# Causal scores as one full float32 product per chunk, instead of three passes over split operands

## The reference

```python
q = rope(x @ Wq.T); k = rope(x @ Wk.T); v = x @ Wv.T
scores = einsum('bhnid,bhnjd->bhnij', qc, kc)        # i, j within a chunk
decay = where(i >= j, exp(G[i] - G[j]), 0)
y_intra = (scores * decay) @ (v * dt)
y_inter = (qc * exp(G)) @ state                       # state from the chunks before
y = rmsnorm(y_intra + y_inter) * gnorm_w * silu(x @ Wg.T)
out = y @ Wo.T
```

## Time and profile before

| what | value |
|---|---|
| median of three runs | 1941.15 us (1938.84 to 1943.4) |
| profiled execution, its own time | 1941.0 us |
| its span, first to last instruction | 1939.2 us |
| TensorE busy | 1832.8 us |
| VectorE busy | 1270.4 us |
| ScalarE busy | 693.4 us |
| GpSimd busy | 643.0 us |

### The profile page before, as it was taken

The page is one execution under the profiler, slowest core; times in us unless marked ns, Lnnn a source line. Parts: engine busy times, 40 slices in busy tenths (PEclk is TensorE's granted clock), DMA queues, the critical chain, the costliest instruction groups (busy, mean ns, idle before and its releaser), DMA issues. The chain is left out here.

```text
span 1939.2 us, 27787 instructions
## 1 busy us (share of the span) xinstructions
PE 1832.8 (95%) x8856; PEld 1482.9 (76%) x8856; DVE 1270.4 (66%) x2340; ACT 693.4 (36%) x2186; POOL 643.0 (33%) x741
## 2 busy tenths in 40 slices
PE   6799999999999999999999999999887999999997
PEld 5588777777777777777777778777766888888885
DVE  7777777787777777777777777777764333333332
ACT  4533443343344434334444434343443112112111
POOL 3444444444444444443444444344400010110100
PEclk9899999999999999999999999999988999999998
DMA  4132332223232223323322232322454322323321
GB/s 153 50 99 83 91 93 70 67 98 92 82 90 94 71 66 93 95 83 91 93 63 70 87 104 77 94 64 63 135 174 155 99 83 81 98 81 92 98 76 33
DMA packets 111073, 173.54 MB, mean 89 GB/s; under 512 B 8016, under 2 KB 45904, under 8 KB 110928
## 3 DMA queue, kind: packets, MB, share of 16 engines
q1 hardware_dynamic: 110928, 171.80, 29.6%
HBM read 133.50 MB, written 38.27 MB: 89 GB/s over the span
## 5 line engine op out<-in xcount | busy, mean ns | idle before, releaser
L84 PE MATMUL p_proj<-wg_hi,shared 128*128 128x512 f32 x1024 | 362.8, 435 | 0.0
L84 PE MATMUL p_proj<-shared,wq_hi 128*128 128x512 f32 x992 | 340.5, 405 | 20.3 <-DVE rope_b L105 20.3
L113 POOL TENSOR_TENSOR q<-rope_a,rope_b 128x512 f32<-128x512 f32 x128 | 165.8, 1295 | 348.8 <-DVE rope_b L105 248.8
L84 PEld LDWEIGHTS p_proj<-wg_hi,shared 128*128 128x128 f32 x1024 | 194.2, 190 | 85.5 <-issue 46.5
L911 ACT ACTIVATE tanh<-p_proj 128x512 f32<-128x512 f32 x128 | 76.6, 599 | 488.5 <-PE p_proj L84 488.5
L84 PEld LDWEIGHTS p_proj<-shared,wq_hi 128*128 128x128 f32 x992 | 189.5, 191 | 69.4 <-DVE rope_b L105 25.5
L84 PE MATMUL p_proj<-wg_lo,shared 128*128 128x512 f32 x512 | 203.3, 397 | 0.0
L84 PE MATMUL p_proj<-shared,wq_lo 128*128 128x512 f32 x496 | 198.6, 400 | 0.0
L84 PE MATMUL p_proj<-shared,wkv_hi 128*128 128x512 f32 x496 | 169.4, 402 | 18.3 <-DVE rope_b L105 18.3
L687 PE MATMUL p_y<-v_tok,probs 128*128 128x128 f32 x1024 | 182.1, 275 | 0.0
L904 ACT ACTIVATE probs<-g_row,stab 128x128 f32<-128x128 f32 x512 | 164.6, 406 | 33.2 <-POOL g_row L1018 33.2
(11 more groups left out here) (181 smaller groups left out, 3711.3 us busy)
## 6 DMA issues: line engine op xcount, KB each, us to landing
g_row<-g_scratch SPq DMA_DIRECT2D x128, 256.0 KB, 6.0
z_scratch<-z_st SPq DMA_DIRECT2D x256, 128.0 KB
w_raw<-z_scratch SPq DMA_DIRECT2D x63, 512.0 KB, 5.9
e_row<-e_scratch SPq DMA_DIRECT2D x96, 256.0 KB, 3.9
w_raw<-in_wq_t SPq DMA_DIRECT2D x16, 512.0 KB, 8.2
w_raw<-in_wg_t SPq DMA_DIRECT2D x16, 512.0 KB, 5.6
w_raw<-in_wo_t SPq DMA_DIRECT2D x11, 512.0 KB, 5.8
w_raw<-in_wkv_t SPq DMA_DIRECT2D x8, 512.0 KB, 5.0
```

The source lines that it names most:

```text
L84: mm = pe.matmul(out, lhs[a], rhs[e], start=(i == 0 and j == 0), stop=(i == len(pairs) - 1 and j == 2))
L113: pool.tensor_tensor(out, keep["rope_a"][:, s, :], keep["rope_b"][:, s, :], ALU.add).then_inc(keep["roped"], 1)
```

## The change

The three products of `scores` become one product of float32 operands, read from `k` and `q` where GpSimd wrote them. The copies and subtractions that split q and k (`q_high`, `k_high`, `q_low`, `k_low`), their buffers and their four semaphores go. `scores` waits for `roped` itself, at chunk 0 of a step, for all five tiles. All else stays in its order.

```diff
-        q_part = [sb(f"q_{e}", [P, HG, C], F32R) for e in ("hi", "lo")]
-        k_part = [sb(f"k_{e}", [P, L], F32R) for e in ("hi", "lo")]
...
-            def scores(n, c):
+            def scores(n, b, c):
                 m = NC * n + c
                 if c == 0:
-                    pe.wait_ge(k_lo_set, n + 1)
+                    pe.wait_ge(roped, ROPED * (n + 1))
                 wait_ge(pe, probs_set, m)
-                pe.wait_ge(q_lo_set, m + 1)
                 at = slice(c * C, (c + 1) * C)
-                wide(pe, p_score[:, :, :], [([w[:, at] for w in k_part], [w[:, :, :] for w in q_part])]).then_inc(score_done, 1)
+                pe.matmul(p_score[:, :, :], k[:, b % 2, at], q[b % 2][:, :, at], start=True, stop=True).then_inc(score_done, 1)
...
-            def k_low(n, b):
-
-                dve.wait_ge(k_hi_set, n + 1)
-                dve.tensor_tensor(k_part[1][:, :], k[:, b % 2, :], k_part[0][:, :].bitcast(F32), ALU.subtract).then_inc(k_lo_set, 1)
-
-            def q_low(n, b, c):
-
-                dve.wait_ge(q_hi_set, NC * n + c + 1)
-                dve.tensor_tensor(q_part[1][:, :, :], q[b % 2][:, :, c * C:(c + 1) * C], q_part[0][:, :, :].bitcast(F32),
-                                  ALU.subtract).then_inc(q_lo_set, 1)
...
-            def q_high(n, b, c):
-                if c == 0:
-                    act.wait_ge(roped, ROPED * (n + 1))
-                wait_ge(act, score_done, NC * n + c)
-                act.activation(q_part[0][:, :, :], q[b % 2][:, :, c * C:(c + 1) * C], ACT.Copy).then_inc(q_hi_set, 1)
-
-            def k_high(n, b):
-                act.wait_ge(roped, ROPED * n + 1)
-                wait_ge(act, score_done, NC * n)
-                act.activation(k_part[0][:, :], k[:, b % 2, :], ACT.Copy).then_inc(k_hi_set, 1)
```

More of the change, by code:

```diff
@@ L478, in attention_stage @@
         masked_set, xw_set = sem("masked_set"), sem("xw_set")
-        q_hi_set, q_lo_set, k_hi_set, k_lo_set = sem("q_hi_set"), sem("q_lo_set"), sem("k_hi_set"), sem("k_lo_set")
         svar_set, srstd_set, stab_set, const_set = sem("svar_set"), sem("srstd_set"), sem("stab_set"), sem("const_set")
@@ L706, in step @@
             def step(g, b, n):
-                scores(n, 0)
+                scores(n, b, 0)
                 next_unit(g, b, n, K_UNIT)
@@ L712, in step @@
                 for c in (1, 2):
-                    scores(n, c)
+                    scores(n, b, c)
                     next_unit(g, b, n, Q_UNIT[c - 1])
@@ L720, in step @@
                 next_unit(g, b, n, Q_UNIT[2])
-                scores(n, 3)
+                scores(n, b, 3)
                 next_unit(g, b, n, Q_UNIT[3])
@@ L764, in first @@
                 dve.memset(eps4[:, :], 4.0 * EPS).then_inc(const_set, 1)
-                k_low(0, 0)
-                q_low(0, 0, 0)
             def make_gate(g, b, n, c):
@@ L838, in step @@
                 make_probs(n, 0)
-                q_low(n, b, 1)
                 if has_last(n):
@@ L854, in step @@
                     scale_q(g, b, n, c)
-                    q_low(n, b, c + 1)
                     make_z(n, c - 1)
@@ L870, in step @@
                 turn_z(n, 2)
-                if ahead(n):
-                    k_low(n + 1, b + 1)
                 make_gate(g, b, n, 3)
@@ L875, in step @@
                     g_low_weights(g + 1, 1)
-                if ahead(n):
-                    q_low(n + 1, b + 1, 0)
                 if group_ahead(g) and b == B - 1:
@@ L949, in first @@
             def first():
-                k_high(0, 0)
                 save_k(0)
-                q_high(0, 0, 0)
                 save_v(0)
@@ L963, in step @@
                     squares(n - 1, 3)
-                q_high(n, b, 1)
                 make_decay(n, b, 1)
@@ L974, in step @@
                     squares(n, c - 1)
-                    q_high(n, b, c + 1)
                     make_decay(n, b, c + 1)
@@ L982, in step @@
                 if ahead(n):
-                    k_high(n + 1, b + 1)
                     make_decay(n + 1, b + 1, 0)
@@ L989, in step @@
                         half_high(wg, 1, wg_hi, 2 * g + 2)
-                    q_high(n + 1, b + 1, 0)
                     save_v_rows(n, b)
```

## The result

The changed kernel takes 1944.99 us in the median (1942.32 to 1947.7), the kernel before, run beside it, 1942.03 (1935.72 to 1944.49). The ratio is 1.0016, with an interval of 1.001 to 1.0023: some 3 us slower, inside the 0.2% that the prediction counts as no change. 1943.8 was forecast. The profiled execution took 1945.15 us, of which 1943.3 are the span: 4.1 more than the profiled execution before.

A forecast was written before the change was run, and what follows sets the result against it. TensorE, busy 95% of the span, was taken to set the pace. The sum 10.5 - 4.3 - 3.4 = +2.8 us on the profiled 1941.0 us gave 1943.8 us, with a range of 1938.5 to 1949.5 (the forecast's own 1940.4 to 1948.9).

The forecast's parts named there:

- the mechanism that was called likeliest: Attention scores: dearer product, 58 of 128 scores hidden, part of the cost given back; +2.8 us in all, chance 0.62.
- The product: Each score on TensorE: one float32 product takes 0.85 us against 0.70 for three float32r passes, 0.15 us more.
- two records of 603 ns laid end to end: Upper bound for each score's product on TensorE: 1.21 us, or 0.5 us more for each score.
- The rival of four passes at 0.233 us: Scores on TensorE: float32 product costs 0.23 us more each, +8.4 us in all, 1949.4 us; chance 0.15.
- The hidden scores: Scores followed by TensorE waits with ends fixed earlier: 58 of 128 cost nothing, 70 exposed cost 10.5 us.
- The v turn: TensorE at the ends of b = 0 steps: five waits vanish without q_high, giving back 4.3 us.
- The same in the five b = 0 steps with such a wait: Scores 0 and 1 there: z waits 0.32 us for srstd, as in b = 3 steps, so 10 scores are hidden.
- The clock: After the seven long b = 3 waits: two falls of the granted clock instead of four, 3.4 us gained.

The follow-up runs named there:

- E3: The kernel before with a fourth float32r pass, low by low, added to each score product: 1949.32 us, ratio 1.0049.
- F1: The kernel before with the rotation of Q unit 3 put ahead of z 2 on VectorE: 1916.97 us, ratio 0.9875.
- F2: The changed kernel with the rotation of Q unit 3 put ahead of z 2 on VectorE: 1919.92 us, ratio 0.9894 against the kernel before.
- E4: The kernel before with save_v_rows put ahead of q_high on ScalarE, nothing else: 1943.4 us, ratio 1.0007.
- E2: The changed kernel with five small one-column copies a step added on ScalarE: 1944.23 us, ratio 1.0021 against the kernel before.
- E1: The kernel before with only the float32 product put in, the splits of q and k kept but unread: 1946.62 us, ratio 1.004.
- G4: The changed kernel with two small copies a step added on ScalarE: 1943.69 us, ratio 1.0007 against the kernel before.

## Why the prediction was right, and where it was not

The total came out as forecast, 1.2 us from the median, and the mechanism that was called likeliest, a dearer product partly hidden and partly paid back, is the one that happened. That it came so close is luck: two terms were wrong, with opposite signs. Step by step:

- **The product.** 0.15 us more for each score was the step; 0.165 was measured, by 0.50 us in a step with three exposed scores. Reading the length from the starts of a product of the same kind was right, and its two records of 603 ns laid end to end would have been too long by 0.35 us. That q is read in pieces costs nothing that shows. The rival of four passes at 0.233 us is excluded for the float32 product, and E3 prices it: 0.07 us above the float32 one. The Trainium skill, FP8 and Floating Point Precision, section "TensorE Precision Notes", states that true float32 takes four passes through the array. The trace fits that, 0.85 us is four times 0.214, though it shows two records for a product and no passes one by one. By the Trainium skill, TensorE: Matmul & The Clock Gate, section "Wait — 56ns, not 53.3ns?", cited in the prediction, a product of 512 columns takes 216 ns. That fits these passes and not the float32r ones, at 233 ns; the Trainium skill names no operand type there. The prediction used this pace for the fourth pass alone and set it beside the rival of four dear passes. Taken for all four it gives 0.86 us, an estimate, or 0.16 more than the three passes' 0.70, and so it pointed to what was measured.
- **The hidden scores.** The 31 scores ahead of the V unit and the 14 of the b = 3 steps are hidden as worked out: the waits went from 0.61 to 0.47 us and from 2.36 to 2.00. F1 and F2 show the cover by removing it: without those waits the distance of an ordinary step grows by 0.15 us.
- **The v turn.** All its waits went and no wait for `roped` came; -5.4 us with restarts, where the prediction took the 4.3 of the waits alone. E4 shows the second cause behind the first, as the step named it (what is late next is the addition).
- **"The same in the five b = 0 steps with such a wait": this step failed.** It took srstd to hold z there as in step 15, with the subtraction in its shadow, and counted ten scores as hidden. But srstd was late because ScalarE stood 2.17 us for "issue" ahead of the squares, and the earlier trace rows showed only that z waited, not why srstd was late. For b = 3 the chain was followed back to the v turn; for b = 0 it was assumed to be the same. With the shorter list the gap went, and five waits with it: -5.2 us, and the ten scores cost 1.65. E2 shows the cause by bringing gaps and waits back.
- **The clock: the term had the wrong sign.** Two falls in place of four were taken, -3.4 us; in the traces there were six, +3.1. A wait shorter by 0.36 us did not mean fewer falls. Over the kernels of this study the number runs from none to six with no order in the length of the waits: 6, 3, 3 and 5 in the changed kernel, E1, E2 and G4, whose longest wait for the rotations is 2.0 us in each. Since executions of one kernel differ as much, the +3.1 holds for the two profiled executions; the medians lie 3.0 us apart where these lie 4.1, and how many falls a typical run has of either wasn't counted. The prediction's own range went from no fall to five, so six lay outside it, and the term should have been carried as unknown in both directions.

Against the forecast's +2.8 the profiled difference was +4.1. The way from one to the other: 70 scores at 0.165 instead of 0.15, +1.0; the v turn -1.1; the five b = 0 steps -5.2 + 1.65 = -3.6; the clock +6.5; outside steps 0 to 30 -1.7, and step 0 +0.4 (the last two largely the clock of the start and the last step). These add to +1.5 where +1.3 is needed. So two misses of 3.6 and 6.5 us with opposite signs stand inside a total that is 1.2 us off.

## What to carry to other kernels

Removing work from engines that don't set the time gives nothing by itself; what it may give sits in the few places where such an engine ends a wait, and these must be followed back to their first cause, "issue" gaps included. A dearer product that looks cheap because a wait covers it becomes its full price once someone removes the wait: the change cost 3 us here and 11.5 us in the kernel with the waits gone, while the same waits removed by reordering and by moving a load brought 54 us. Where the clock falls after some waits and not after others, and differently from one execution to the next, compare kernels by the length of undisturbed steps and by their lists of waits, and put the falls into the range in both directions.

## What the runs showed that was not expected

- At the turn of the loop ScalarE stands 2.2 to 2.4 us for "issue" or not at all, by the length of its list: gaps with 78 or 79 packets on the queue of instructions, none with 52 or 54. Two more instructions a step than the changed kernel has left it at none, five brought the gaps back; one fewer than the kernel before did not remove them. VectorE's gap of 1.9 us stayed. Two packets of instructions come in the stretch of each of ScalarE's gaps, and one where only VectorE stands. Where between two and five instructions the limit lies, and whether the fetch is the cause, was not tried.
- Four float32r passes take 0.07 us longer than one full float32 product of the same shape (steps of 41.92 and 41.71 us).
- Once the clock falls in one group it falls in each following group at the same distance in the traces of the kernel before (four) and of the changed kernel (six, 170.7 us apart, the group's length). It is no rule: in G4, with steps of the same length, it falls in three groups, then in two not, then in two again. What decides it stays open.
